# A graph network on one core: w_hh is turned before the first input, the first state products take their high parts first, and later loads are asked for behind half of the first adjacency

## The reference

```python
A = (adj != 0).astype(x.dtype)
h = x
for l in range(5):
    m = jnp.einsum('bnd,de->bne', h, weight[l])
    agg = jnp.einsum('bij,bid->bjd', A, m)
    gi, gh = agg @ w_ih.T + b_ih, h @ w_hh.T + b_hh      # each split in r, z, n
    r, z = sigmoid(i_r + h_r), sigmoid(i_z + h_z)
    n = tanh(i_n + r * h_n)
    h = (1 - z) * n + z * h
x = layernorm(x + h * mask)
x = layernorm(x + second_network(x, adj))
```

## Time and profile before

| | us |
|---|---|
| median of 3 runs (493.0 to 493.22) | 493.06 |
| the profiled execution | 493.06 |
| its span | 491.3 |
| TensorE busy | 480.5 (98%) |
| VectorE busy | 352.4 (72%) |
| ScalarE busy | 303.6 (62%) |
| GpSimd busy | 334.5 (68%) |

### The profile page before, as it was taken

How to read it: one execution, slowest core, us unless ns; L and a number is a source line. 1 busy time by engine, 2 the same in 40 slices (tenths; PEclk the granted TensorE clock), 3 DMA queues, 4 the chain that set the end, 5 groups by cost and what they waited for, 6 DMA issues and landing times.

```text
span 491.3 us, 7178 instructions
## 1 busy us (share of the span) xinstructions
PE 480.5 (98%) x2301; PEld 229.6 (47%) x2301; DVE 352.4 (72%) x659; ACT 303.6 (62%) x537; POOL 334.5 (68%) x378
## 2 busy tenths in 40 slices
PE   7999999999999999999999999999999999999994
PEld 5444444444444444444444444444444444564554
DVE  3777867696867687778587777877668675445796
ACT  4556655655655656776657775576765776655564
POOL 3654774748775698997689748659996776334466
PEclk9999999999999999999999999999999999999998
DMA  8878252565535537264955476323443233322313
GB/s 271 258 172 157 45 150 54 151 155 140 120 63 151 118 88 184 57 142 107 175 112 163 106 211 166 73 43 77 89 106 83 57 65 63 65 43 42 83 45 86
DMA packets 133676, 55.72 MB, mean 113 GB/s; under 512 B 97297, under 2 KB 125414, under 8 KB 133638
## 3 DMA queue, kind: packets, MB, share of 16 engines
q1 hardware_dynamic: 108356, 32.39, 32.1%
q10 hardware_dynamic: 25282, 22.87, 14.9%
HBM read 27.46 MB, written 4.19 MB: 64 GB/s over the span
## 4 chain that ended last, share of the span: by engine, by line
PE 83%; POOL 6%; DVE 3%; DMA 3%; ACT 2%; issue 2%; POOLq 0%; DVEq 0%; ACTq 0%
PE pA L790 24%; PE pR L795 6%; PE pR L797 6%; PE pR L796 6%; PE pZ L797 6%; PE pZ L796 6%; PE pZ L795 6%; PE pIN L795 3%; PE pHN L795 3%; PE pHN L796 3%; PE pHN L797 3%; PE pIN L797 3%; PE pIN L796 3%; POOL ZH L528 2%; POOL HT L539 1%
## 5 line engine op out<-in xcount | busy, mean ns | idle before, releaser
L539 POOL TENSOR_TENSOR HT<-H,HT 128x512 f16<-128x512 f32 x76 | 91.8, 1208 | 90.1 <-ACT HT L1167 90.1
L790 PE MATMUL pA<-A,NAT 128*128 128x512 fp8e4 x640 | 151.0, 379 | 0.0
L528 POOL TENSOR_TENSOR ZH<-Z,H 128x512 f32<-128x512 f32 (+1 forms) x80 | 102.6, 1283 | 28.7 <-ACT Z L1182 27.2
L1422 DVE SCALAR_TENSOR_TENSOR T<-pHN,BHN,R 128x512 f32<-128x512 f32 (+1 forms) x80 | 59.9, 749 | 78.2 <-ACT R L1174 77.8
L1187 ACT ACTIVATE pIN<-T,COLS 128x512 f32<-128x512 f32 (+1 forms) x80 | 55.2, 691 | 71.1 <-DVE T L1426 71.0
L790 PEld LDWEIGHTS pA<-A,NAT 128*128 128x128 f16 x640 | 62.5, 98 | 74.8 <-issue 1.0
L1167 ACT ACTIVATE HT<-H 128x512 f16<-128x512 f32 x76 | 47.8, 628 | 64.8 <-DVE H L1436 64.6
L1432 DVE SCALAR_TENSOR_TENSOR pIN<-Z,pIN 128x512 f32<-128x512 f32 (+1 forms) x80 | 55.1, 689 | 24.4 <-ACT pIN L1187 24.2
L1174 ACT ACTIVATE R<-pR,BRZ 128x512 f32<-128x512 f32 (+1 forms) x80 | 54.3, 679 | 20.1 <-PE pR L797 19.4
L1436 DVE TENSOR_TENSOR H<-ZH,pIN 128x512 f32<-128x512 f32 (+1 forms) x80 | 54.8, 685 | 10.1 <-POOL ZH L528 7.7
L1416 DVE TENSOR_TENSOR AG<-pA,AG 128x512 f16<-128x512 f32 x80 | 54.7, 684 | 7.7 <-ACT AG L1163 7.7
(11 more groups left out here) (284 smaller groups left out, 810.1 us busy)
## 6 DMA issues: line engine op xcount, KB each, us to landing
AS<-in_adj_dram ACTq DMA_DIRECT2D x13, 1024.0 KB, 5.9
XR<-in_x_dram ACTq DMA_DIRECT2D x16, 256.0 KB, 2.9
XS<-in_x_dram ACTq DMA_DIRECT2D x13, 256.0 KB, 3.3
out_dram<-Y SPq DMA_DIRECT2D x16, 192.0 KB, 2.2
AS<-in_adj_dram SPq DMA_DIRECT2D x2, 1024.0 KB, 8.7
AS<-in_adj_dram SPq DMA_DIRECT2D x4, 256.0 KB, 5.4
NAT<-HT SPq DMA_TRANSPOSE x64, 3.2
XS<-in_x_dram SPq DMA_DIRECT2D x3, 256.0 KB, 7.8
```

Of the source, the lines that this page charges most:

```text
L528: g_.tensor_tensor(ZH[:, cs], Z[:, cs], H[:, b, cs], ALU.mult).then_inc(zh_p, 1)
L539: g_.tensor_tensor(HT[:, b, 1, :], H[:, b, :], HT[:, b, 0, :], ALU.subtract).then_inc(h_lo, 1)
L790: last = mm(pA2[:, k % 2, :], NAT[:, k % 2, h, i, :], A8[:, b, i, :], start=(h == 0 and i == 0), stop=(h == 1 and i == NI - 1))
L1422: v.scalar_tensor_tensor(out=T[:, cs], in0=pHN[:, cs], scalar=BHN[:, 0:1], in1=R[:, cs], op0=ALU.add, op1=ALU.mult).then_inc(t_v, 1)
```

## The change

Four edits, all at the start. SP waits for block 1 of adjacency 0 (the second of four) in place of w_ih and weight 0 before it asks for the later data. TensorE turns w_hh ahead of x(0). ScalarE casts w_hh first, then HT(0), then copies w_ih, and makes NAT(0)'s high half last of these; VectorE makes the low half of w_hh before that of HT(0). And in first_gates_of_state the products with w_hh's low half come before those with x's low half.

```diff
@@ sync
-            sp.wait_ge(ld_wi, 32)
+            sp.wait_ge(ld_a0[1], 16)
             load_x(1)
             load_a(1)
@@ tensor, first_gates_of_state
                 pe.wait_ge(wh_hi, 1)
                 for bank, g in banks:
                     mm(bank[:, :], WH[:, 0, g, :], hi, start=True, stop=False)
+                pe.wait_ge(wh_lo, 1)
+                for bank, g in banks:
+                    mm(bank[:, :], WH[:, 1, g, :], hi, start=False, stop=False)
                 pe.wait_ge(x_lo, 1)
                 for bank, g in banks:
-                    mm(bank[:, :], WH[:, 0, g, :], lo, start=False, stop=False)
-                pe.wait_ge(wh_lo, 1)
-                for bank, g in banks:
-                    mm(bank[:, :], WH[:, 1, g, :], hi, start=False, stop=(bank is pHN))
+                    mm(bank[:, :], WH[:, 0, g, :], lo, start=False, stop=(bank is pHN))
@@ tensor
-            transpose_x(0, pF)
             pe.wait_ge(ld_wh, 16)
             for g in range(3):
                 last = tr(pA2[:, 1, g * D:(g + 1) * D], WHS[:, g, :], IDF[:, :])
             last.then_inc(wh_t, 1)
+            transpose_x(0, pF)
             pe.wait_ge(ld_wi, 32)
@@ scalar
-            natural_hi(0)
-            transposed_hi(0, pF)
             act.wait_ge(wh_t, 1)
             fn(WH[:, 0, :, :].rearrange("p g d -> p (g d)"), pA2[:, 1, 0:3 * D], ACT.Copy,
                scale=WSCALE).then_inc(wh_hi, 1)
+            transposed_hi(0, pF)
             act.wait_ge(wi_t, 1)
             fn(WT, pIN[:, :], ACT.Copy).then_inc(wi_v, 1)
+            natural_hi(0)
             merged_hi(0, pIN)
@@ vector
-            transposed_lo(0, pF)
             dve.wait_ge(wh_hi, 1)
             split_lo(WH[:, 0, :, :], WH[:, 1, :, :], pA2[:, 1, :]).then_inc(wh_lo, 1)
+            transposed_lo(0, pF)
             cast_first(0)
```

## The result

The changed kernel takes 496.82 us (median of 5 runs, 496.27 to 498.18) against 493.0 us for the kernel before (5 runs): +3.8 us, a ratio of 1.008 with a 95% interval of 1.0065 to 1.0094. The profiled execution took 498.18 us, the slowest of the five, with a span of 496.4 us, 5.1 us over the span before: what is read from it explains more than the 3.8 us of the median.

What follows compares the result with a forecast made beforehand. TensorE was taken as the bound, its start set by its own work and HT(2)'s landing. Late x(1) and a(1), in parallel, +0.6 and HT(2) +0.15 gave +0.75 on 493.06: 493.8 us, range 492.6 to 495.1.

Steps and rivals of the forecast that it cites:

- The bound and the reading: Whole kernel: TensorE bounds it; a shift reaches the end only if TensorE's own work and HT(2)'s landing both move.
- w_hh first, high parts first: Start of TensorE: w_hh's transposes fit before x(0), no waits; first product at 6.94 us, 0.37 us earlier.
- Rival 3: Start of TensorE: w_hh's transposes quicken those of x(0), 0.4 us earlier; at best -1.0; 492.55 us, chance 0.08.
- natural_hi behind the rest: Before the first aggregation: later natural_hi(0) leaves 0.17 of 0.37 us gained, aggregation at 9.19; bounds -0.37 to +0.2.
- side branch of rival 1: Casts 1 to 3 of adjacency 0 held by GpSimd's natural_lo(0) and first_state(0): up to +0.6 us.
- rival 1: Before aggregate(1)'s second half: late a(1)'s second cast waits for GpSimd's kept_share(0); +1.8 us, 494.9 us, chance 0.24.
- x(1): ScalarE's natural_hi(1): x(1) lands after 3.3 us at 11.4, putting AG at 11.9; +0.6 us.
- a(1): VectorE's casts before aggregate(1): a(1) lands after 5.9 us at 14.4, aggregate(1) at 15.25; +0.6, parallel to x(1)'s.
- The transposing DMA: HT(2) behind a(3) and the deferred loads: 0 to 0.4 us more, taken as +0.15, landing about 23.8 us.
- Rival 2: Deferred loads as fast as the best or faster: x(1) by 10.9, a(1) by 13.9; -0.1, 492.95 us, chance 0.18.
- four signs of being wrong: x(1) before 10.8 us; a(1)'s second cast over 1 us; w_hh after x(0); a(3) not ahead of HT(2).

Runs made afterwards that it cites:

- e1_sp_only: Kernel before with only the SP edit (later loads wait for block 1 of adjacency 0): 495.17 us against 493.21, ratio 1.0043.
- e3: Changed kernel loading only the first of four blocks of graph 3's adjacency, a(3): 493.25 us against 493.21 for the kernel before, ratio 1.0005.
- e5: Changed kernel with ScalarE asking for a(3) only behind SP's request for HT(2): 493.38 us, against 496.55 for the changed kernel and 493.04 for the kernel before.
- e11: Changed kernel with x(1), a(1) asked for at the old place, only the later loads deferred: 493.41 us against 493.08 for the kernel before, ratio 1.0007.
- e4_fill: Changed kernel with twelve extra products on TensorE right before its wait for HT(2): 496.13 us against 493.21 for the kernel before, ratio 1.006.
- e10_after_again: Changed kernel run again, unaltered, on another chip: 496.55 us, ratio 1.0067 against the kernel before.
- e6: Kernel before with a(3) asked for late, behind HT(2), and none of the change: 492.36 us against 493.04, ratio 0.9986.
- e7: Changed kernel with SP's old wait, natural_hi(0) in ScalarE's gap before HT(0), and a(3) asked for late: 492.22 us against 493.04 for the kernel before.
- e9: Changed kernel with SP waiting for block 3 of adjacency 0, not block 1: 496.71 us against 493.08 for the kernel before, ratio 1.0075.

## Why the prediction was wrong

**The bound and the reading.** That TensorE's belt starts with the wait for HT(2), and that every delay ahead of it is carried to the end, held: the changed kernel is 4.95 us late at 30 us and 5.1 at the end of the span, TensorE being busy in all of the stretch from 40 to 100 us.

**w_hh first, high parts first.** Held. The first product came at 6.67 us, even earlier than the 6.94 forecast, because the transposes of w_hh ran before x(0) landed, those of x(0) began at 4.94, so that HT(0) was ready at 6.61 and not 6.79, and the product followed 0.06 us after it, not 0.15. The order cost nothing in waiting. Rival 3 asked whether w_hh's transposes would quicken those of x(0): they took 1.04 us against 1.07, so it did not come.

**natural_hi behind the rest.** Its start was right (9.06 against 9.19) and the gain was lost as feared in the range, by the mechanism named as a side branch of rival 1: the four casts of adjacency 0 took 3.35 us beside GpSimd, and aggregate(0) stopped for 0.5 us. I had put +0.6 at most on it and nothing in the sum. AG went at 11.71; the forecast had 11.9, for another reason, so that this number is near is luck. For x(1) took only 2.6 us, not 3.3, and was not what was waited for.

**a(1).** Landing near 14.3 against 14.4, aggregate(1) at 15.30 against 15.25. Held, in that run; e1_sp_only shows a run with 7.2 us in place of 5.9.

**The transposing DMA.** This is the step that failed. The forecast took 0 to 0.4 us, +0.15 in the sum, for what was left of the deferred 3 MB in front of HT(2), and the wait became 2.6 us longer. In the start of HT(2)'s packets that term was near (3.7 us after the request, 3.6 before). What had no term is how a(3) and HT(2) end: a(3) was taken to need its usual time, and it needed 8.2 us in place of 5.6, the last two of them one engine's, with half of HT(2) behind them. The deferral was costed at the two loads that have a waiter near, x(1) and a(1), and the stream behind them was taken as nearly caught up; but the engines were full before (339 to 362 GB/s from 7 to 10 us), so SP's loads ended at 19.9 us in place of 18.2, and a(3) started among them. In the median, loading only a quarter of a(3) (e3), asking for it behind HT(2) (e5) or keeping the engines fed (e11) takes the loss away. How the crowded start of a(3) leaves one engine two microseconds behind is open.

**The clock.** Not in the forecast at all: a wait of 3.1 us turned into a further 1.6 us at half the clock. The Trainium skill, "TensorE: Matmul & The Clock Gate", Part 1, says that the array falls back to half rate when it has been idle and needs work to come back; the stretches here agree, with 0.50 from 27 to 29 us after the wait, 1.00 again from 30 us, and 1.00 throughout in e4_fill. A rival with a long wait in it should have carried that price.

**Rivals and range.** Rival 1 had the right sign, but +1.8 us, by a late a(1) whose cast meets kept_share. The changed kernel's profile shows none of it: its two casts took 1.29 us. e1_sp_only's does: a(1) took 7.2 us, the cast begun at 15.61 ended 0.55 us after kept_share(0) did, as in the earlier trace rows, only it was the first cast and not the second, and TensorE waited 2.2 us. Rival 2, loads at least as fast as the best, was right for x(1) (2.6 us) and useless for the time: the estimate from the fit in the Trainium skill's "DMA: Bandwidth & Descriptors", section on the anatomy of one DMA (2.6 us for 256 KB, for GpSimd's path), agrees with this one load, while a(1) took 5.8 us against its 4.4. Of the four signs of being wrong one came, x(1) before 10.8 us (10.67), and it pointed to a faster kernel; the other three stayed away while the time left the range. The range ended at 495.1 because the price of the queue was bounded by the landing of single loads, never by the bytes that would not be moved or by two transfers that end together.

## What to carry to other kernels

When a request is put off, count what the DMA engines carry in that stretch: if they are full, the bytes not moved stand in front of what follows until a slack stretch takes them up, and they can hurt first at a wait 15 us later and on another queue, as here. Put the one transfer that TensorE waits for ahead of the megabyte nobody needs yet; one wait did that here and gave 0.7 us in the kernel before and 3.2 in the median of the changed one. It must be well ahead: in the runs here 1.1 us was enough and 0.4 us was not. And price a long wait of TensorE with its clock.

## What the runs showed of the hardware that was not expected

A transposing DMA from SP stood behind an ordinary load from ScalarE, on another queue, until that load's last engine was through: 8.33 us from request to landing in the changed kernel, 7.7 in e10_after_again and e4_fill. Half of its packets went ahead of that end and half behind it. Asked for 1.1 us ahead of the load (e5, e6, e7), it took 3.2 to 3.6 us; asked for only 0.4 us ahead (e1, e9), it took 6.4 and 6.5 us, its packets going slowly beside the load's. Why a single engine is behind by two microseconds was not found.

A tiny operation can be held as a large one is. VectorE's sum of two bias columns, two columns wide (L1664), took 0.99 us in the changed kernel against 0.16 before; it ended when GpSimd's natural_lo(1), from 11.38 for 1.16 us, ended. The Trainium skill, "GPSIMD Engine Reference", section 1, names VectorE's instructions with two SBUF inputs beside those in a 2-port mode as the ones that contend with GpSimd; the 0.99 us agree, and the prediction had thought only of the casts. It put AG's low half from 12.3 to 12.54.
